# Attention on one core: the next head pair's Q product inside the current step, and both heads' values products side by side

## The reference, cut to what matters

```python
q, k, v = split((shift_token(x)) @ wqkv)           # 8 heads of 64
q, k = rotary_xpos(l2norm(q) * qs, l2norm(k) * ks)
out = local_attention(q, k, v)                     # windows of 64 tokens, each sees itself and the one before
x = x + out @ wo
h = layernorm(shift_token(x)) @ w1 + b1            # hidden size 341, twice
a, g = split(h)
x = x + (a * gelu(g)) @ w2 + b2
```

## Time and profile before

| | us |
|---|---|
| median of 3 runs | 1157.02 |
| lowest and highest run | 1152.47, 1161.21 |
| span of the profiled execution, first to last instruction | 1152.9 |
| TensorE matmul busy in it | 995.2 |
| VectorE, ScalarE, GpSimd busy | 719.8, 681.6, 514.8 |

### The profile page before, as it was taken

How to read it: one execution, slowest core, us unless ns; L and a number is a source line. 1 busy time by engine, 2 the same in 40 slices (tenths; PEclk the granted TensorE clock), 3 DMA queues, 4 the chain that set the end, 5 groups by cost and what they waited for, 6 DMA issues and landing times.

```text
span 1152.9 us, 26028 instructions
## 1 busy us (share of the span) xinstructions
PE 995.2 (86%) x9072; PEld 628.5 (55%) x9072; DVE 719.8 (62%) x1657; ACT 681.6 (59%) x1311; POOL 514.8 (45%) x392
## 2 busy tenths in 40 slices
PE   4789999999998877789999999999829986856995
PEld 1445555555555347255555555556418983535995
DVE  1568677778777554477777777778674432665442
ACT  3566686686684572666676676674616654633662
POOL 2455456456442524455553453452463550363552
PEclk9989999999999987899999999999958997776998
DMA  5665454354434600444443443443422222012224
GB/s 177 159 154 135 123 146 112 91 131 112 93 94 99 78 1 3 92 112 112 111 106 86 106 111 85 102 111 75 150 89 61 67 71 74 18 49 63 61 67 128
DMA packets 89711, 109.99 MB, mean 95 GB/s; under 512 B 20368, under 2 KB 74384, under 8 KB 88816
## 3 DMA queue, kind: packets, MB, share of 16 engines
q1 hardware_dynamic: 82160, 91.17, 33.5%
q0 software_dynamic: 4544, 9.35, 2.3%
q10 hardware_dynamic: 2880, 7.81, 2.2%
HBM read 62.66 MB, written 12.07 MB: 65 GB/s over the span
## 4 chain that ended last, share of the span: by engine, by line
PE 66%; ACT 15%; issue 7%; DVE 6%; DMA 3%; POOL 2%; SPq 1%; ACTq 0%; DVEq 0%; POOLq 0%
PE banks L589 7%; PE banks L936 6%; PE banks L946 6%; PE banks L662 5%; PE banks L676 5%; PE banks L620 4%; PE banks L751 3%; PE banks L669 3%; PE banks L637 3%; PE banks L726 2%; PE banks L721 2%; PE banks L645 2%; ACT arena L1184 2%; ACT arena L1189 2%; PE banks L971 1%
## 5 line engine op out<-in xcount | busy, mean ns | idle before, releaser
L2062 POOL TENSOR_TENSOR arena<-arena 128x1024 f32<-128x1024 f32 x64 | 150.9, 2358 | 323.7 <-DVE arena L1662 317.4
L2051 POOL TENSOR_TENSOR arena<-arena 128x1024 f32<-128x1024 f32 x64 | 150.9, 2357 | 40.8 <-ACT arena L1184 40.8
L1654 DVE TENSOR_REDUCE arena<-banks 128x4 f32<-128x512 f32 x128 | 82.4, 685 | 95.1 <-PE banks L620 95.0
L1176 ACT ACTIVATE arena<-banks,arena 128x512 f32<-128x512 f32 x128 | 80.5, 679 | 92.0 <-PE banks L669 91.5
L589 PE MATMUL banks<-arena 128*128 128x512 f32 x256 | 127.2, 621 | 6.7 <-DVE arena L1554 5.9
L2041 POOL DMA_INDIRECT moe_outs<-arena x78 | 81.2, 1040 | 98.2 <-DVE arena L1904 94.1
L1397 ACT ACTIVATE arena<-banks,arena 128x128 f32<-128x128 f32 x312 | 89.0, 369 | 55.8 <-PE banks L936 55.5
L2034 POOL DMA_INDIRECT moe_rows<-arena x64 | 63.9, 998 | 94.6 <-DVE arena L1635 70.3
L1662 DVE TENSOR_TENSOR arena<-arena 128x1024 f32<-128x1024 f32 x64 | 78.0, 1219 | 24.6 <-DMA arena<-arena 24.6
L1189 ACT ACTIVATE arena<-banks 128x1024 f32<-128x1024 f32 x64 | 65.6, 1025 | 44.8 <-PE banks L589 43.9
L946 PE MATMUL banks<-arena 128*128 x624 | 86.7, 282 | 3.5 <-ACT arena L1397 2.9
(11 more groups left out here) (220 smaller groups left out, 1914.5 us busy)
## 6 DMA issues: line engine op xcount, KB each, us to landing
arena<-arena SPq DMA_DIRECT2D x256, 128.0 KB, 3.9
arena<-rstd SPq DMA_DIRECT2D x128, 256.0 KB, 4.2
arena<-moe_rows SPq DMA_DIRECT2D x78, 64.5 KB
arena<-in_mw SPq DMA_DIRECT2D x2, 2048.0 KB, 11.5
arena<-moe_outs SPq DMA_DIRECT2D x16, 256.0 KB, 4.8
arena<-in_rot ACTq DMA_DIRECT2D x12, 256.0 KB, 3.2
arena<-in_wa ACTq DMA_DIRECT2D x2, 1026.0 KB, 6.7
arena<-ssm_a SPq DMA_DIRECT2D x4, 512.0 KB, 6.6
```

The costliest lines, as they stand in the source:

```text
L1654: nc.vector.tensor_reduce(mx[:, e], by_row(bank[3 + e][:]), AX.X, ALU.max).then_inc(s_max, 1)
L2051: nc.gpsimd.tensor_tensor(TA[:, n % 2], RAW, ROTV[:, :, 0, c * C:(c + 1) * C], ALU.mult).then_inc(cos_done, 1)
L2062: nc.gpsimd.tensor_tensor(TA[:, n % 2], TA[:, n % 2], TB, ALU.add).then_inc(rot_sum, 1)
```

## The change

Q and K are no longer made together. `project(s, k)` makes one of them. K of step s stands at the head of step s. Q of step s+1 stands in step s: between the centred block and the variance (hp 0, and steps 4 and 5), behind the first gate and value pair (hp 1), in the middle of the four V products (hp 2), between `mlp_output` and `output` (hp 3), and behind the scores in the other early steps. All its waits go with it, for the `copied` of both halves of step s too. The second head's values products stand right behind the first's in every step but step 32.

```diff
             def ffn(norm0, run):
-                def project(s, n):
-                    hp, c, d = s % HP, s // HP % NCH, s // (HP * NCH)
-                    if d == 0:
-                        need(pe, ln_out, norm0 + c + 1)
-                    else:
-                        pe.wait_ge(mlp_out, 2 * NCH * run + c + 1)
-                    if run == 0 and s % (HP * NCH) == 0:
-                        pe.wait_ge(wa_in[d], 16)
-                    after(pe, copied, 2 * n)
-                    src = (YA, YM)[d][:, c * C:(c + 1) * C]
-                    for k in range(2):
-                        w0 = k * INNER + hp * P
-                        mm(bank[k], w_qkv[d][:, w0:w0 + P], src, start=True, stop=True).then_inc(proj, 1)
+                def project(s, k):
+
+                    if s >= STEPS:
+                        return
+                    n, hp, c, d = STEPS * run + s, s % HP, s // HP % NCH, s // (HP * NCH)
+                    if k == 0:
+                        if d == 0:
+                            need(pe, ln_out, norm0 + c + 1)
+                        else:
+                            pe.wait_ge(mlp_out, 2 * NCH * run + c + 1)
+                        if run == 0 and s % (HP * NCH) == 0:
+                            pe.wait_ge(wa_in[d], 16)
+                        after(pe, copied, 2 * n)
+                    w0 = k * INNER + hp * P
+                    mm(bank[k], w_qkv[d][:, w0:w0 + P], (YA, YM)[d][:, c * C:(c + 1) * C],
+                       start=True, stop=True).then_inc(proj, 1)
...
-                def project_v(g, s):
+                def project_v(g, s, t0):
                     d, c, gg = g // NCH, g % NCH, 2 * NCH * run + g
-                    for t in range(TILES):
+                    for t in range(t0, t0 + 2):
...
                     mm(bank[7][:], centre, YB[:, c * C:(c + 1) * C], start=True, stop=True).then_inc(mn_cen, 1)
-                    values(s - 3, STEPS * run + s - 3, 1)
                     if s < STEPS:
+                        project(s + 1, 0)
                         pe.wait_ge(ss_log, STEPS * run + s + 1)
                     else:
+                        values(s - 3, STEPS * run + s - 3, 1)
                         bank2_read(pe, run, s)
...
                     first_centred(norm0, c, run)
-                    values(s - 3, STEPS * run + s - 3, 1)
+                    project(s + 1, 0)
                     pe.wait_ge(ss_log, STEPS * run + s + 1)
...
-                    if s < STEPS:
-                        project(s, n)
-                    elif run:
+                    if s == 0:
+                        project(0, 0)
+                    project(s, 1)
+                    if s == STEPS and run:
...
-                    filled = g >= 2 and hp in (1, 3) or hp == 2 and s >= 6
                     if s >= 3:
                         values(s - 3, n - 3, 0)
-                    if filled:
-                        values(s - 3, n - 3, 1)
+                        if s < STEPS:
+                            values(s - 3, n - 3, 1)
...
-                    elif s >= 3 and not filled:
-                        values(s - 3, n - 3, 1)
                     if hp == 1 and g >= 2:
-                        for j in range(3):
-                            hidden(g - 2, s, j)
+                        hidden(g - 2, s, 0)
+                        project(s + 1, 0)
+                        hidden(g - 2, s, 1)
+                        hidden(g - 2, s, 2)
                     if hp == 2:
-                        project_v(g, s)
+                        project_v(g, s, 0)
+                        project(s + 1, 0)
+                        project_v(g, s, 2)
                     if hp == 3 and g >= 2:
                         mlp_output(g - 2, s)
+                    if hp == 3:
+                        project(s + 1, 0)
                     if hp == 3 and g >= 1:
                         output(g - 1, s)
+                    if hp < 2 and g < 2 and s not in (4, 5):
+                        project(s + 1, 0)
                     if s >= 2:
                         transpose_scores(s - 2, n - 2)
```

## The result

The changed kernel takes 1167.37 us (median of 4 runs, 1164.4 to 1172.66), the kernel before 1155.3 with its fourth run. The ratio is 1.0098, 95% interval 1.0059 to 1.0137: 1% slower, as forecast. The profiled execution was the longest of the four (1172.66; its span is 1170.8). In the new file a line of TensorE's part is 2 to 4 higher than before (L589 is L591, L596 is L599, L637 is L640, L721 is L725) and one of ScalarE's or VectorE's is 10 higher (L1694 is L1704). Steps are named H0 to H3 as in the prediction, T is the start of the L591 row at a step's head.

A forecast was written before the change was run, and what follows sets the result against it. TensorE's queue was taken as the path, with late bank 7 readers and V's copy replacing Q's cover. Terms -7.2, +0.3, +5.0, +8.6, +3.8 and +0.6 gave +11.1 on 1157.0: 1168.1 us, range 1160 to 1175.

The forecast's parts named there:

- H0: Steps with s mod 4 = 0: shorter head, Q fills the gap before the variance; 8.57 to 7.97 us, -7.2 over twelve.
- H1: Steps with s mod 4 = 1: transposes wait for bank 7, Q overfills the gate gap; +0.03 each, +0.3 in all.
- H2: Steps with s mod 4 = 2: square sum 0.42 earlier (first pass 0.09), Q among V products costs 0.71; +5.0 together.
- H3: Steps with s mod 4 = 3: values still wait for V's shifted copy, Q costs its full 0.86; +8.6 over ten.
- first steps: Early steps of both passes, through step 7: Q's cost and waits for evacuation or V's copy; +1.9 per pass, +3.8.
- restart: TensorE starting again behind the V copy: 0.16 taken instead of 0.11, +0.05 on twelve steps, +0.6.
- its wait: First pass, 4.27 us TensorE wait at 59.59, chain back to transfers: claimed to absorb the costs of steps 2 and 3.
- only the V copy binds: Rival: bank 7 waits do not bind in steps with hp 1 and 2, the square's end does; 1162 us, chance 0.11.
- the square alone binds: Rival: the square is the only late comer at the heads, V's copy keeps up; 1148 us, chance 0.08.
- dearer stops: Rival: each of some 36 new TensorE stops adds 0.15; +5.4, giving 1173.5 us, chance 0.15.
- The clock: Rival: new idle time, up to 0.9 us a step, lowers TensorE's granted clock; above 1190 us, chance 0.02.
- an inserted product is free: Rival: idle time lies inside the matmul rows, so added products cost nothing; -10.6, giving 1146.4 us, chance 0.01.

The follow-up runs named there:

- e8_only_q2_early: Kernel before, with only Q of the steps with hp 2 moved behind the first gate and value pair of the step before; 1153.59 us in one execution.
- the first experiment, e1: Changed kernel, with Q of the steps with hp 3 back at the head of its own step; ratio to the kernel before 1.0005.
- e5_values_first: Changed kernel, with the values products ahead of the output transposes in steps with hp 1 and 2 from step 4 on; 1156.49 us in one execution.
- e4: Changed kernel, with the two parts of V's shifted copy on VectorE in the other order; ratio to the kernel before 1.0012.
- e3: Changed kernel with the values edit undone: Q early, values products where the kernel before has them; 1174.63 us in one execution.
- e6: Changed kernel, with V's copy in the other order and values ahead of the transposes in hp 1 and 2; ratio to before 0.995, median 1149.98 us.
- e7: Kernel before, with the two parts of V's shifted copy in the other order and nothing else; 1150.84 us in one execution.

## Why the prediction was right

The forecast was 1168.1 and the measured median 1167.37; as a difference, 11.1 forecast and 12.1 between the medians, a ratio of 1.0096 forecast and 1.0098 measured. That the two times lie within 1 us is in part luck: the kernel before came out 1.7 lower with its fourth run, the terms below miss by 1.2 the other way, and single executions of one kernel spread by more than either. What was right is where the time goes. Term by term, from the two profiles:

| term | forecast | measured |
|---|---|---|
| H0, twelve | -7.2 | 8.57 to 8.02, -6.5 |
| H1 | +0.3 | +0.04 or less each, +0.3 |
| H2 | +5.0 | +0.30 six times; +0.62 four times, 0.48, 0.30: +5.1 |
| H3, ten | +8.6 | 12.17 to 13.03 or 13.04, +8.7 |
| first steps, both passes | +3.8 | +4.8 |
| restart | +0.6 | in H3 none: 0.10 behind the copy |
| sum | +11.1 | +12.3 |

The first steps are steps 2 to 7. Steps 0 and 1, the start of the first pass and the stretch between the passes stand in no row: they add 1.6 and take 1.6 off. That pair is no work of the change, for the trace of e8_only_q2_early, whose code in these steps is the old one, has it too (between the passes 119.75 us, steps 0 and 1 of the second pass 14.50; before 121.25 and 13.18, changed 119.86 and 14.43).

**H0** gives 0.05 less than reckoned each time, 0.7 in all: its square sum stands at T+2.51, not 2.46. The transposes start at 0.87 and take 0.56 here. VectorE's residual, the bank 7 reader of that step, ends at T+0.72, so here too the bank is only just free; the prediction left this reader out.

**H1.** Transposes at T+1.64, square sum at T+3.29, second gate product at T+7.76, against 1.64, 3.27 and 7.74. The gap was filled; the time that K left at the head went to the wait before the transposes, which the kernel before does not show in steps 8 to 31.

**H2.** Transposes at T+1.29, square sum at T+2.93, Q at 0.71 net. The 0.71 was shown by itself, in the first experiment.

**H3** went as reckoned, and its reason was tried from both sides.

**First steps.** Here lies the largest error, and in single steps it is larger than in the sum. Step 2 of the second pass came out at +1.17 where +0.71 was forecast. The 0.71 is right: in the trace of e5_values_first, whose code in this step is the same, it is 10.76 against 10.06, +0.70. The rest is Q and K at its head: their row takes 2.99 us at a granted clock of 0.62, between the two levels of 1.2 and 2.4 GHz, and 1.88 at 1.00 in e5_values_first and before. The first two rows are from the changed kernel, the last two from e5_values_first; a stretch's row has the columns of the earlier trace rows:

```profile
483.49 2.99 PE L591 MATMUL banks<-arena 128*128 128x512 f32 x4
483.50:486.40 2.90, 2.90 (x5) 0.99 (x3) 1.18 (x2) 1.41 (x2) 1.60 (x2) 0.62 0.68 148
...
478.16 1.88 PE L591 MATMUL banks<-arena 128*128 128x512 f32 x4
478.20:480.00 1.80, 1.80 (x5) 0.53 (x3) 0.17 (x1) 1.41 (x2) 1.78 (x2) 1.00 1.03 224
```

The traces of e1 and e4 have the low clock in that step too, those of e3 and e6, which also have Q early, don't; whether the change brings it about is open. Step 4 of the second pass came out at 8.94, -0.37 and not -0.86, since ScalarE's copy of Q and K, earlier now, waits 0.36 for the transfer that empties its buffer. ScalarE's timeline of that step, T at 503.24:

```profile
504.36 1.02 ACT L1199 ACTIVATE arena<-banks 128x1024 f32<-128x1024 f32 x1 [0.23 <-PE banks L591]
505.74 1.27 ACT L1194 ACTIVATE arena<-banks,arena 128x512 f32<-128x512 f32 x2 [0.36 <-DMA arena<-arena]
```

The square did come 0.85 earlier, at T+1.12 instead of T+1.97. What failed is the second half of "the square comes 0.86 earlier and with it all that ScalarE does": the copy behind it came 0.39 earlier, and so did the output's evacuation (T+4.58 instead of T+4.96). Steps 5, 6 and 7 came at +0.48, +0.70 and +0.43 (0.46, 0.71, 0.44 forecast), step 3 of the second pass at +0.24 instead of 0.47. In the first pass steps 2 and 3 added 1.2 and step 4 gave 0.6 back. Whether its wait absorbed that can't be told: the step lasts 15.37 us before and 14.76 changed, and 13.20 and 15.27 in the two experiments on the kernel before that leave it alone (e7 and e8).

**The rivals.** That only the V copy binds falls with the waits of 0.62 and 0.26. That the square alone binds falls with H3's 13.03. The dearer stops do not show: 0.10 to 0.15 from releaser to matmul, with the one exception that the prediction knew, step 3 of the second pass, 0.26 there. The clock stayed at 1.00 through steps 8 to 30 of both passes. That an inserted product is free falls with the 0.71 and the 0.86 it cost. The page Perfetto Trace Analysis of the Trainium skill, in its section Identifying the Most-Contended Engine, names two measures to use in place of matmul busy time, MFU (the share of the peak FLOP rate) and the weight loads' share; the prediction took up the second alone, and nothing here works out the first. The weight loads' share by itself would have misled: with float32 products of 512 columns the queue was full while weight loads covered 27.30 of 50 us.

## What to carry to other kernels

Before a product is moved out of a step's head, list every wait that stands behind it in the queue and the time each is released, counted from the step's start: what was covered by the product becomes the new start, and the waits list of the kernel before does not hold these entries. An early placement pays where two things meet, a gap at the new place and nothing else late at the old one; H2's Q is the one that was shown to pay when moved alone, and H3's met neither. And look for the releaser that a reorder on its own engine sets free: a copy in the other order was worth 10 of the 12 us that the change cost.

## What the runs showed that was not expected

A shortened head laid bare waits within a few hundredths of the end of the old cover: V's copy at its cover's end in the kernel before, and in H0 the residual 0.15 before the transposes of the changed one. From step 8 of the second pass on, the profile put all six waits before the values down to "issue", each ending 0.10 after VectorE's copy, and with the copy earlier they were gone: idle time with that label was here a wait for another engine. The same wait in step 3 it put down to L1704. The values of one head take 0.62 us, of both side by side 1.08, so the second costs 0.46 there.
